# Sums over eight moved to TensorE transposes, and the down product of eleven experts in float32r, in a 256-chunk expert kernel

## The reference

```python
x = x + attn_a(ln(x))    # r * (first * kv + state), state = kv + decay * state, norm, Wo
x = x + ffn(ln(x))       # 8 experts, 512 hidden
x = x + attn_b(ln(x))    # 16 heads with an 8x8 state each
x = x + ffn(ln(x))       # the same experts again
```

```python
tmp = einsum('bhj,bhjk->bhk', a * knt, wkv)                    # a sum over 8
wkv = d[..., None] * wkv - knt[..., None] * tmp[:, :, None, :] + vt[..., None] * rk[:, :, None, :]
out = einsum('bhij,bhj->bhi', wkv, rt)                          # a sum over 8
```

```python
h = silu(einsum('bsh,ehf->ebsf', x, w_gate)) * einsum('bsh,ehf->ebsf', x, w_up)
out = einsum('ebsh,bse->bsh', einsum('ebsf,efh->ebsh', h, w_down), cw)
```

## Time and profile before

| | us |
|---|---|
| median of 3 runs | 852.18 (852.18 to 852.9) |
| the profiled execution | 851.54 |
| its span, first to last instruction | 849.8 |

### The profile page before, as it was taken

The page is one execution under the profiler, slowest core; times in us unless marked ns, Lnnn a source line. Parts: engine busy times, 40 slices in busy tenths (PEclk is TensorE's granted clock), DMA queues, the critical chain, the costliest instruction groups (busy, mean ns, idle before and its releaser), DMA issues. The chain is left out here.

```text
span 849.8 us, 12968 instructions
## 1 busy us (share of the span) xinstructions
PE 778.9 (92%) x4610; PEld 655.0 (77%) x4610; DVE 616.7 (73%) x1224; ACT 361.1 (42%) x740; POOL 343.7 (40%) x296
## 2 busy tenths in 40 slices
PE   7999999999889889997888698889999899999997
PEld 5977988888767778676576577777788678878886
DVE  6699565278988876679989999987768778443333
ACT  5242244653483235563233375144333444364332
POOL 4453201066446945523356572864344324211000
PEclk9999999999999999997899899999999999999999
DMA  9500000011011151141410011143223310000000
GB/s 285 135 2 2 1 1 1 1 50 51 0 50 51 51 149 51 42 130 53 124 47 30 25 69 31 53 108 94 58 88 112 100 38 25 1 2 13 1 1 13
DMA packets 27447, 45.38 MB, mean 53 GB/s; under 512 B 7504, under 2 KB 14328, under 8 KB 27384
## 3 DMA queue, kind: packets, MB, share of 16 engines
q1 hardware_dynamic: 27384, 44.56, 17.3%
HBM read 29.88 MB, written 14.68 MB: 52 GB/s over the span
## 5 line engine op out<-in xcount | busy, mean ns | idle before, releaser
L1376 PEld LDWEIGHTS bank<-w_down,sh_buf 128*128 128x128 f32 x2048 | 269.9, 196 | 64.2 <-DVE sh_buf L1902 42.2
L1376 PE MATMUL bank<-w_down,sh_buf 128*128 128x128 f32 x2048 | 281.3, 281 | 31.3 <-DVE sh_buf L1902 31.1
L1186 ACT ACTIVATE sh_buf<-bank 128x512 f32<-128x512 f32 x256 | 152.4, 597 | 282.0 <-PE bank L1376 192.1
L1902 DVE TENSOR_TENSOR sh_buf<-sh_buf,bank 128x512 f32<-128x512 f32 x256 | 171.9, 682 | 122.3 <-PE bank L1376 97.4
L1376 PE MATMUL bank<-z_hi,w_lo 128*128 128x512 f32 x512 | 225.0, 439 | 1.5 <-ACT z_hi L1166 0.8
L1376 PE MATMUL bank<-z_lo,w_hi 128*128 128x512 f32 x512 | 204.4, 399 | 7.6 <-DVE z_lo L1913 7.6
L1376 PE MATMUL bank<-z_hi,w_hi 128*128 128x512 f32 x512 | 203.8, 398 | 0.0
L1070 POOL TENSOR_TENSOR x<-x,y_weighted 128x512 f32<-128x512 f32 x41 | 53.4, 1303 | 192.9 <-ACT y_weighted L1309 192.9
L1376 PEld LDWEIGHTS bank<-z_lo,w_hi 128*128 128x128 f32 x512 | 97.4, 190 | 31.7 <-DVE z_lo L1913 8.8
L1376 PEld LDWEIGHTS bank<-z_hi,w_lo 128*128 128x128 f32 x512 | 99.0, 193 | 17.9 <-issue 3.7
L1376 PEld LDWEIGHTS bank<-z_hi,w_hi 128*128 128x128 f32 x512 | 98.5, 192 | 13.0 <-issue 0.5
(11 more groups left out here) (228 smaller groups left out, 950.1 us busy)
## 6 DMA issues: line engine op xcount, KB each, us to landing
trans_spill<-state SPq DMA_DIRECT2D x16, 512.0 KB, 2.6
backs<-chain_spill SPq DMA_DIRECT2D x16, 512.0 KB, 4.8
backs<-trans_spill SPq DMA_DIRECT2D x16, 512.0 KB, 3.3
backs<-keep_spill SPq DMA_DIRECT2D x4, 1024.0 KB, 5.6
x<-in_x SPq DMA_DIRECT2D x4, 256.0 KB, 5.6
backs<-in_w_gate SPq DMA_DIRECT2D x4, 256.0 KB, 5.6
backs<-in_w_up SPq DMA_DIRECT2D x4, 256.0 KB, 5.8
keep_spill<-rkv SPq DMA_DIRECT2D x4, 256.0 KB, 2.7
```

Source lines behind the costliest of these rows:

```text
L1186: act.activation(s_buf[:, m % 2, :], bank_of("gate", m)[:], ACT.Silu).then_inc(S["silu_done"], 1)
L1376: return pe.matmul(dst, lhs, rhs, start=start, stop=stop, **kw)
L1902: dve.tensor_tensor(h_buf[:, m % 4, :], s_buf[:, m % 2, :], bank_of("up", m)[:], ALU.mult).then_inc(S["h_done"], 1)
```

## The change

It has five parts.

1. **Sums.** Three new tables by block say where the sums of the readout (`READS` = 0, 1, 1, 1), of `y0` (`Y0S` = 0, 1, 1, 0) and of `y1` (`Y1S` = 1, 1, 0, 0) are made. Where they are 1, eight transposes accumulate into a bank (`turned_every`); their weights are every eighth column of the product, where `turned_sum` has 128 neighbouring columns. That is 12 + 8 + 8 = 28 sums. Reads and y1 are copied by ScalarE while turned and turned back four at a time (`turned_block`: 3 + 2 groups of four transposes), and `block_end` and `back_sum` read them from the bank. A y0 is turned back by itself and copied a second time, since `through` on GpSimd reads it.
2. **PE_SUMS.** T2 of steps 1, 2, 4, 10, 13 and 14 and W2 of 2, 7 and 10 go to VectorE; T2 of 3 and 11 go to TensorE. So 17 of them stay on TensorE, where there were 24.
3. **Down product.** `DOWNS` marks e = 43, 48, 50, 51, 53, 54, 57, 58, 60, 61 and 62. For their 44 chunks ScalarE copies the hidden values rounded (`high`, 128 x 512), VectorE or GpSimd makes the rest (`low`; 20 chunks on VectorE, 24 on GpSimd), and TensorE does three float32r products of 128 x 512 with `down_hi` and `down_lo` as weights. The output has channels on partitions; VectorE weighs it (`turn_weigh`, with weights that come by way of DRAM), GpSimd sums the experts of a pass (`turn_sum`), four transposes turn it and VectorE adds it to `x` once a pass (`turn_add`). Once, `down_hi` (8 copies on ScalarE) and `down_lo` (8 subtractions on GpSimd) are made from `w_down`, in memory that the steps no longer need.
4. **Who does what.** `MULS` has 4 and 4 pieces of the two chains on GpSimd, where it had 6 and 6; `ADDS` is another table; the filler products ahead of the first FFN are 20, where they were 28.
5. **Planner.** Its times, weights and leads are others, it counts 0.13 us between a TensorE result and its reader, and a pass's first gate product now waits in it for `z_lo` (`ffn_low`), as it does in the program.

```diff
-MULS = [[1, 1, 1, 1, 1, 0, 0, 1], [1, 1, 0, 1, 1, 1, 1, 0]]
+MULS = [[0, 1, 1, 0, 1, 1, 0, 0], [1, 0, 1, 0, 0, 1, 1, 0]]
...
-PE_SUMS = dict(T2=[0, 1, 1, 0, 1, 1, 1, 1, 0, 1, 1, 0, 1, 1, 1, 1], W2=[0, 0, 1, 0, 1, 1, 1, 1, 1, 1, 1, 1, 1, 1, 1, 1])
+PE_SUMS = dict(T2=[0, 0, 0, 1, 0, 1, 1, 1, 0, 1, 0, 1, 1, 0, 0, 1], W2=[0, 0, 0, 0, 1, 1, 1, 0, 1, 1, 0, 1, 1, 1, 1, 1])
...
+RING = 3
+READS = [0, 1, 1, 1]
+Y0S = [0, 1, 1, 0]
+Y1S = [1, 1, 0, 0]
-TABLE_LOAD, HOP, START = 1.28, 0.07, 5.0
+TABLE_LOAD, HOP, LATE, START = 1.28, 0.07, 0.13, 5.0
...
         if c == 0:
-            after += (on("act", "ffn_z", q),)
+            after += (on("act", "ffn_z", q), on("dve", "ffn_low", q))
...
-            pe(("mid_out", q), 0.82, *inner, on("pe", "mid_T", q), on("act", "wo"), *((on("pe", "mid_out", q - 1),) if q else ()), takes=((("mid_out", q), on("dve", "mid_add", q)),)),
+            pe(("mid_out", q), 1.9, *inner, on("pe", "mid_T", q), on("act", "wo"), *((on("pe", "mid_out", q - 1),) if q else ()), takes=((("mid_out", q), on("dve", "mid_add", q)),)),
...
+        if READS[j]:
+            out += [pe(("read", t), TURNED_SUM, on("pool", "readout", t), takes=((("read", t), on("act", "read", t)),)),
+                    act(("read", t), 0.28, on("pe", "read", t), *((on("act", "read", t - 1),) if i else ()))]
...
+            def turned_every(bank, product):
+
+                for k in range(N):
+                    ins = pe.matmul(bank[:, 0:P], product.rearrange("p (hi k) -> p k hi", k=N)[:, k], ident[:],
+                                    is_transpose=True, start=(k == 0), stop=(k == N - 1))
+                return ins
...
+            def turned_down(m, half):
...
+                if half == 0:
...
+                    mm(dst, down_lo[:, e % E, f, :], h_hi[:, n % RING, :], start=(f == 0), stop=False)
+                    mm(dst, down_hi[:, e % E, f, :], h_hi[:, n % RING, :], start=False, stop=False)
+                else:
+                    pe.wait_ge(S["h_low_dve" if LOWS[e] else "h_low_pool"], lows(m))
+                    mm(dst, down_hi[:, e % E, f, :], h_lo[:, n % RING, :], start=False,
+                       stop=(f == FC - 1)).then_inc(S["y_full" if f == FC - 1 else "d_done"], 1)
...
+            def turn_weigh(e):
...
+                dve.tensor_tensor(turned_y[:] if first else turned_part[:], bank_of("y", e)[:], cw_wide[:, n % RING, :],
+                                  ALU.mult).then_inc(S["turn_weighed"], 1)
```

More of the change, by code:

```diff
@@ L155, in experts @@
         if g >= 4:
-            after += (on("pe", "down", g - 4, 1),)
+            after += (on(lower(g - 4), "low", g - 4) if DOWNS[(g - 4) // FC] else on("pe", "down", g - 4, 1),)
         if g == 3:
@@ new lines, in experts, with reader @@
+    if turned:
+        last = L - 1
+        freed = (on("dve", "finish", UNITS - 1, 1), on("sp", "keepA", BLOCKS - 1), on("sp", "keepB", BLOCKS - 1), on("sp", "spill", last))
+        for i in range(E):
+            out += [act(("down_hi", i), 0.62, *(freed if i == 0 else (on("act", "down_hi", i - 1),))),
+                    pool(("down_lo", i), 1.3, on("act", "down_hi", i), *((on("pool", "down_lo", i - 1),) if i else ()), port=True)]
+    return out
+def reader(t):
+    return on("pe" if READS[t // G] else "dve", "read", t)
@@ L473, in lead @@
         kind, n = o.key[0], o.key[1:]
-        if kind in ("gate", "up", "silu", "hidden", "down", "high", "low"):
+        if kind in ("gate", "up", "silu", "hidden", "down", "high", "low", "up_copy"):
             return LEAD["experts"][4 * n[0] // CHUNKS]
@@ L497, in start @@
         o = self.ops[k]
-        begin = max([self.now[o.engine]] + [self.end[a] + HOP for a in o.after])
+        begin = max([self.now[o.engine]] + [self.end[a] + HOP + late(a, o.engine) for a in o.after])
         stage, name = self.ln(o)
@@ L541, in release @@
         if o.engine == "sp":
-            begin = max([START] + [self.end[a] for a in o.after])
+            begin = max([START] + [self.end[a] + late(a, "sp") for a in o.after])
             self.sp.append((begin, len(self.sp), o.key))
@@ L816, in weighed, with tokens, written, lows @@
         def weighed(e):
-            return e - sum(ADDS[:e])
+            return sum(not ADDS[i] and not DOWNS[i] for i in range(e))
+        def tokens(flags, t):
+            return sum(flags[i // G] for i in range(t + 1))
+        writes = x_writes()
+        turned = turned_chunks()
+        def written(*write):
+            return writes.index(write) + 1
+        def lows(g):
+            return sum(LOWS[i // FC] == LOWS[g // FC] for i in turned if i <= g)
+        def summed(e):
+            return sum(DOWNS[i] and not is_first(i) for i in range(e))
+        def turned_passes(q):
+            return sum(any(DOWNS[E * i:E * i + E]) for i in range(q))
         def logs(j):
```

493 lines of the change are left out of this document (404 added, 89 removed).

## The result

| | before | after |
|---|---|---|
| median, us | 852.18 (849.64 to 852.9, 4 runs) | 838.12 (835.64 to 838.57, 4 runs) |
| profiled execution, us | 851.54 | 837.91 |
| its span, us | 849.8 | 836.1 |
| mean granted clock | 0.974 | 0.983 |

The ratio of the times is 0.983, 95% interval 0.981 to 0.986: faster by 14 us. The forecast was 838.

The account below looks back on a forecast made before the run. TensorE was taken to bound the ends and link chains, VectorE 248 us between; -10 - 2.1 + 0 + 4.3 - 6.7 = -14.5 us cut the span to 835.3, plus 1.7 and 0.6: forecast 838 us, range 826 to 857.

Parts of the forecast that it names:

- VectorE in its 248 us: Steps and first back parts (251-304, 376-488, 488-571 us): 16.5 us less VectorE work, 10 us of it taken as gain.
- 304 to 376 us: Chain of links beneath TensorE: 5.8 us more on VectorE, no change in time; at most 5.8 late if cover goes.
- Before 251 us: First stretch, TensorE the bound: two sums and their turns back fewer there, -2.1 us; fewer filler products, nothing.
- 571 to 683 us: TensorE gets four y0 sums and two transpose groups, one expert gives back 0.8: +4.3 us.
- 683 us to the end: 40 chunks in float32r at 0.21 us less each, four groups of transposes +1.7: -6.7 us.
- TensorE as the bound: Same 248 us: idle is latency, new TensorE work comes on top; 865 in full, 857 with half in idle; chance 0.19.
- Strided weights: The 28 sums at 0.24 us a step take 1.9 instead of 0.93 us: 849 to 861, centre 855; chance 0.06.
- The clock's return: VectorE's full 16.5 us show and TensorE stays at 2.4 GHz, another 6.5 us go: 826 to 831; chance 0.14.
- No gain: New order loses elsewhere what is gained, with new waits at `high` and `low`; time stays at 852; chance 0.08.
- The signs of being wrong: Block 1's first step to block 3's end taking 320 us or more, or end down products waiting for `h_hi` or `h_lo`.
- The other sign: Down products at the end wait for `h_hi` or `h_lo`; no size given.

Follow-up runs that it names:

- the bonus later: Changed kernel with block 3's four bonus operations (an output term, on VectorE) moved behind the end of the steps, ahead of expert 36's add: 834.61 us.
- that experiment: Changed kernel with the down products of the 11 experts back in float32, without roundings, transposes back and turned-weight loads: 841.76 us.

## Why the prediction was right

**The bound.** Right that it isn't TensorE in the steps: undoing the sums showed it three times over, each time slower with less work on TensorE. VectorE's load is shown as the bound from gate 105 to 131 (13.4 us for 14.5). It is not shown from 131 to 150: there five reads put back on VectorE cost nothing, and with the bonus later 5.7 us less work on it than before left the length at 82.9.

**VectorE in its 248 us, -10 of 16.5.** Measured -11.5, in part by luck. VectorE's busy time fell by 13.8 there (227.8 to 44.88 + 91.05 + 78.06), and TensorE's idle time from 42.2 to 26.5. But the number is a sum of three things that the prediction did not part: full price from gate 105 to 131 (-13.0, for 12.0 us less on VectorE), -6.0 from 70 to 83, which comes back in the next stretch with the work that crossed gate 83, and the misplaced bonus (+7.5). The prediction took 10 of the 16.5 us for want of cover on TensorE, because no stretch had both engines above 90%; from 105 to 131 both are now at 91 to 92% (90.85 and 91.05 of 99.4). So the cover was there, and the loss had another cause. Of the 12 reads that the prediction took off VectorE there, one lay behind gate 150 already. The comparison of the two orders on VectorE around block 3 would have shown the bonus moved from behind the steps into them.

**304 to 376 us, 0.** Measured +6.4. About half of it is an effect of the cuts. The two `starts` products of block 0 (2.0 us), two reads of block 1 with their turn back (2.2) and the down products of chunks 78 to 80 now lie in this stretch; two up products and two and a half down products left it. In sum TensorE is busy for 3.4 us more (67.84 to 71.26). The other 3.0 us are idle time of TensorE (4.3 to 7.3). VectorE is busy for 14.4 us more (47.8 to 62.2), where the prediction had 5.8 of links: a whole step and eight more additions to `x` are in it too. Together with the 6.0 us that the stretch ahead lost, the two are 0.4 us longer than before. What the idle time comes from was not taken apart.

**Before 251 us, -2.1.** Measured -6.2. TensorE's busy time fell by 4.6 and its idle time from 9.3 to 7.2. T2 and W2 are 2.1 of it by their rows, which no run tested, and the filler is at nothing. The other 4 us are in no experiment; the new planner with the old tables was at gate 70 only after 262.9 us, so it is no gain of the planner alone. This stays open.

**571 to 683 us, +4.3.** Measured +3.1, right by luck. The 4.2 us for y0 on TensorE were wrong as a cost: taking the sums back made the stretch 2.4 us longer. TensorE's busy time rose by 6.2 us: the y0 sums, other work that crossed the cut (two `finish_T`, a read and the turn back of block 3's, some 2.2 us) and the transposes for the down products. Its idle time fell from 7.3 to 4.2 us and took half of that.

**683 us to the end, -6.7.** Measured -5.5, of which the down products are 4.7. The step was right and its size too large: 6.7 against 4.7, in part pauses ahead of float32r steps, as that experiment shows.

**The rivals.** TensorE as the bound: it asks for more than 30 us of idle time in the three stretches, and 26.5 were left; the runs with sums back exclude it. Strided weights: excluded by 0.11 us a step. The clock's return: in part true. The clock of the middle stretch went from 0.88 to 0.97, as foreseen, but the last one's fell to 0.92 with the bonus; the kernel with the bonus moved is at 0.96 there. No gain: the new order did lose 7.5 us at one place, of which a better placing gave back 2.0 to 3.5 in the whole, and the rest outweighed it.

**The signs of being wrong.** The part from gate 70 to 150 takes 315.8 us, where it took 320.9: not the 320 or more that would have refuted the prediction, but only 5 us less, with the 7.5 us of the bonus in it. The other sign did come, in small: down products at the end waited 1.0 us for `h_hi` and `h_lo`, and 4.7 of 6.7 us were gained.

**What the forecast owes to luck.** The parts were missed by +6.4, -4.1, -1.5, -1.2 and +1.2 us, 0.8 in sum. 838 was right as a total of errors that cancelled, with the two large steps of the right sign; the first has its size from gains and losses that cancel within it.

## What to carry to other kernels

Find the engine that bounds a stretch, not the program, and move work off that one; from gate 105 to 131 a microsecond of VectorE work was worth nearly a whole one (13.4 for 14.5). A high busy share alone doesn't prove the bound: from 131 to 150 VectorE was at 86 to 93%, and 6.1 us more on it cost nothing. When a planner writes the order, compare stretch by stretch, at the same work items, and check which work crossed a cut before a stretch is read as a gain. The stretch that goes against the trend held the placing loss here, one block of 2.9 us of work that took 6.8 beside GpSimd and cost 7.5. A sum moved to another engine is cheap in its own row and is paid in the queues that it joins.

## What the runs showed of the hardware

- A float32 product of 128x128 with weights read at a stride of 32 bytes took 0.24 us, with adjacent ones 0.11. A transpose took 0.11 at either.
- A VectorE TENSOR_TENSOR with two SBUF inputs of 128x512 took 0.69 us alone, and up to 2.78 when it started beside a GpSimd operation. A reduction with one input took 0.69 beside GpSimd too.
- At a change from float32 to float32r products the first float32r step took 0.32 us instead of 0.23, and the last float32 step ahead of it 0.03 instead of 0.11. In sum the change is nearly free. The change back to float32 showed no price.
